# Attention and a routed feed-forward layer on one core: the front's instructions in a new order on four engines, and the second slot table partly moved between the first three rounds

## The reference

```python
def _L0_conv_ref(x, w_kq, b_kq, w_v, b_v, w_o, b_o):
    xf = x.reshape(B, C, N)
    kq = jnp.einsum('kc,bcn->bkn', w_kq, xf) + b_kq[None, :, None]
    v = jnp.einsum('vc,bcn->bvn', w_v, xf) + b_v[None, :, None]
    sim = jnp.einsum('bkn,bkm->bnm', kq, kq)
    attn = jax.nn.softmax(sim, axis=-1)
    ctx = jnp.einsum('bnm,bvm->bvn', attn, v)
    out = jnp.einsum('ov,bvn->bon', w_o, ctx) + b_o[None, :, None]
    ...
def _L0_ffn_ref(x, router_w, w1, w2, w3):
    logits = flat @ router_w.T
    probs = jax.nn.softmax(logits, axis=-1)
    topk_probs, topk_idx = jax.lax.top_k(probs, TOP_K)
    topk_probs = topk_probs / (jnp.sum(topk_probs, axis=-1, keepdims=True) + 1e-09)
    ...
    h = jax.nn.silu(h1) * h3
    y = jnp.einsum('neh,ech->nec', h, w2)
    out = jnp.einsum('ne,nec->nc', gates, y)
...
x = x + _L0_conv_ref(_ln_c(x), ...)
t = _to_tokens(x)
t = t + _L0_ffn_ref(_ln_t(t), ...)
```

## Time and profile before

| | us |
|---|---|
| median of 3 runs | 176.22 |
| lowest, highest | 175.45, 176.61 |
| the profiled execution's own time | 174.48 |
| its span (first to last instruction) | 172.7 |
| PE busy | 143.8 |
| DVE busy | 100.6 |
| POOL busy | 85.8 |
| ACT busy | 71.4 |

### The profile page before, as it was taken

The page is one execution under the profiler, slowest core; times in us unless marked ns, Lnnn a source line. Parts: engine busy times, 40 slices in busy tenths (PEclk is TensorE's granted clock), DMA queues, the critical chain, the costliest instruction groups (busy, mean ns, idle before and its releaser), DMA issues.

```text
span 172.7 us, 4880 instructions
## 1 busy us (share of the span) xinstructions
PE 143.8 (83%) x1682; PEld 120.2 (70%) x1682; DVE 100.6 (58%) x372; ACT 71.4 (41%) x141; POOL 85.8 (50%) x114
## 2 busy tenths in 40 slices
PE   1589849488788678996999999999999999983871
PEld 1356737277376258896798989999999999872271
DVE  1636695785853988869764656464555654532050
ACT  2347666141144044353363636363636354541021
POOL 2695237877770577773262626253444444466000
PEclk9999987955555589999999999999999999999698
DMA  4999300001872691298978889696949871010524
GB/s 136 313 292 295 101 0 23 27 15 35 268 308 48 217 348 52 58 320 296 318 278 275 323 258 344 235 358 184 393 111 395 266 281 37 9 34 16 160 106 109
DMA packets 19893, 33.00 MB, mean 191 GB/s; under 512 B 7691, under 2 KB 13100, under 8 KB 19868
## 3 DMA queue, kind: packets, MB, share of 16 engines
q1 hardware_dynamic: 16732, 29.55, 52.1%
q0 software_dynamic: 2272, 2.35, 4.1%
q10 hardware_dynamic: 864, 0.79, 1.4%
HBM read 25.55 MB, written 7.13 MB: 189 GB/s over the span
## 4 chain that ended last, share of the span: by engine, by line
PE 62%; DVE 9%; DMA 8%; issue 6%; ACT 5%; POOL 5%; SPq 1%; POOLq 1%; ACTq 0%; DVEq 0%
PE psum L1035 21%; PE psum L1063 12%; PE psum L929 7%; PE psum L918 4%; PE psum L1017 3%; POOL xs L361 3%; PE psum L898 3%; ACT xn L430 2%; DMA y_in<-ys 2%; PE psum L1041 2%; DMA x_in<-xs 2%; POOL ys L374 2%; PE psum L1107 2%; PE psum L889 2%; DVE hid L831 2%
## 5 line engine op out<-in xcount | busy, mean ns | idle before, releaser
L374 POOL DMA_INDIRECT ys<-y_out,y_row x39 | 37.4, 958 | 44.9 <-DVE hid L831 39.8
L831 DVE TENSOR_TENSOR hid<-psum,act_sb 128x512 f32<-128x512 f32 (+1 forms) x50 | 33.7, 677 | 29.4 <-ACT act_sb L508 28.7
L1035 PE MATMUL psum<-x_cols,weights 64*128 64x128 f32 x390 | 49.7, 279 | 0.3 <-ACT x_cols L500 0.2
L1037 PE MATMUL psum<-x_cols,weights 64*128 64x128 f32 x390 | 49.8, 279 | 0.0
L1035 PEld LDWEIGHTS psum<-x_cols,weights 64*128 64x128 f32 x390 | 45.6, 188 | 4.5 <-issue 2.2
L1037 PEld LDWEIGHTS psum<-x_cols,weights 64*128 64x128 f32 x390 | 45.6, 187 | 0.0
L508 ACT ACTIVATE act_sb<-psum 128x512 f32<-128x512 f32 (+1 forms) x50 | 29.3, 586 | 23.9 <-PE psum L1035 23.9
L361 POOL DMA_INDIRECT xs<-xrows,pos x32 | 31.7, 989 | 11.6 <-issue 8.9
L1063 PE MATMUL psum<-hid,weights 128*64 128x128 f32 x468 | 28.8, 276 | 0.2 <-DVE hid L831 0.2
L1063 PEld LDWEIGHTS psum<-hid,weights 128*64 128x64 f32 x468 | 25.9, 137 | 2.0 <-DVE hid L831 0.4
L929 PEld LDWEIGHTS psum<-u_sb,probsT 128*128 128x128 f32 x64 | 11.4, 268 | 5.2 <-ACT probsT L464 2.8
(11 more groups left out here) (148 smaller groups left out, 179.1 us busy)
## 6 DMA issues: line engine op xcount, KB each, us to landing
weights<-experts SPq DMA_DIRECT2D x39, 565.0 KB, 5.6
xs<-zeros SPq DMA_DIRECT2D x4, 1040.0 KB, 12.0
x_in<-xs SPq DMA_DIRECT2D x39, 32.5 KB
ys<-y_out,y_row POOLq DMA_INDIRECT x39
xs<-xrows,pos POOLq DMA_INDIRECT x32, 2.6
y_in<-ys ACTq DMA_DIRECT2D x2, 256.0 KB, 4.6
y_in<-ys SPq DMA_DIRECT2D x2, 256.0 KB, 4.4
x_sb<-x_tok SPq DMA_DIRECT2D x1, 384.0 KB, 3.6
```

Source lines behind the costliest of these rows:

```text
L374: nc.gpsimd.indirect_dma_start(ys, bass.IndirectOffsetOnAxis(ap=y_row[:, j:j + 1], axis=0), y_out[:, i % RING, h, :], None).then_inc(y_sca ...
L831: nc.vector.tensor_tensor(live(i, hid[:, i % 2, s, :]), live(i, H3_BANK[g % 3]), live(i, act_sb[:, g % 3, :]), ALU.mult).then_inc(hid_done, 1)
L1035: first_ = nc.tensor.matmul(H1_BANK[g % 2][:, src], weights[0:C, slot, P * s:P * (s + 1)], x_cols[0:C, i % 2, src], start=True, stop=True)
L1037: second_ = nc.tensor.matmul(H3_BANK[g % 3][:, src], weights[C:P, slot, P * s:P * (s + 1)], x_cols[C:P, i % 2, src], start=True, stop=True)
```

## The change

The work is the same; its order is another.

- PE: the similarities of the next pair stand between a pair's two attentions, not after them. `rank(p-1)` stands behind `value_out(p)` and also waits for the copy of these values. Transposes and keys of the pair after next stand at the pair's end. There are 23 `keep_busy` products in place of 14 up to the first quad.
- ACT: `xT_copy` moves behind the second image's probsT copy, next to `kq_copy`.
- DVE: `row_max` of the next pair's first image stands before the second residual, that of its second image before `positions`. The first table is split around residual(4), tops(4) and row_max(6). Behind the front, `rows_of_slots(1)`, `normalise_t(3)` and the parts of the third table move to places between the multiplies of quads 0, 1 and 2; `pair_up(2)` moves into quad 1.
- POOL: `t_deviation` stands before another scatter. `turn_x(2)` on PE and its copy on ACT move from quad 1's step 0 to its step 4.

```diff
+DEVIATION_AT = (4, 5, 3)
...
+        def turns_at(i):
+            return {0: 1, 1: 4}.get(i, 0)
...
             for p in range(PAIRS):
                 for at in range(TPP * K_TOP):
-                    if p == 0 and at == TPP * K_TOP - 2 or p == 2 and at == K_TOP:
+                    if p + 1 < PAIRS and at == DEVIATION_AT[p]:
                         t_deviation(p + 1)
                     scatter_row(p, at)
-                if p == 1:
-                    t_deviation(2)
...
                 u_copy(p)
-                if p + 2 < PAIRS:
-                    xT_copy(p + 2)
                 exponentials(2 * p + 1)
                 probsT_copy(2 * p + 1)
                 if p + 2 < PAIRS:
+                    xT_copy(p + 2)
                     kq_copy(p + 2)
...
             for p in range(PAIRS):
+                last = p == PAIRS - 1
+                if p >= 1:
+                    x_logits(p)
                 if p == KNOWN[0]:
                     subtiles_of_experts(0)
+                residual(2 * p)
+                tops(2 * p)
+                if not last:
+                    row_max(2 * p + 2)
+                if p == KNOWN[0]:
                     owners_of_slots(0)
                     rows_of_slots(0)
-                if p >= 1:
-                    x_logits(p)
-                residual(2 * p)
-                tops(2 * p)
                 residual(2 * p + 1)
                 t_statistics(p)
-                if p + 1 < PAIRS:
-                    row_max(2 * p + 2)
                 tops(2 * p + 1)
                 choose(p)
-                carry_on(p)
-                if p == PAIRS - 1:
+                if last:
                     pair_up(0)
+                else:
+                    carry_on(p)
+                    row_max(2 * p + 3)
                 positions(p)
-                if p == PAIRS - 1:
-                    used_up(0)
-                    subtiles_of_experts(1)
-                    owners_of_slots(1)
-                    rows_of_slots(1)
-                    pair_up(1)
-                normalise_t(p)
-                if p + 1 < PAIRS:
-                    row_max(2 * p + 3)
+                if not last:
+                    normalise_t(p)
+            pair_up(1)
+            used_up(0)
+            subtiles_of_experts(1)
+            owners_of_slots(1)
...
             def tables_between(i, s):
-                if (i, s) == (0, 5):
+                if (i, s) == (0, 1):
+                    rows_of_slots(1)
+                elif (i, s) == (0, 5):
+                    normalise_t(PAIRS - 1)
+                elif (i, s) == (1, 1):
                     used_up(1)
+                elif (i, s) == (1, 2):
                     subtiles_of_experts(2)
-                elif (i, s) == (1, 1):
+                elif (i, s) == (1, 5):
                     owners_of_slots(2)
-                elif (i, s) == (1, 3):
+                elif (i, s) == (2, 1):
                     rows_of_slots(2)
-                elif (i, s) == (1, 5):
+                elif (i, s) == (2, 5):
                     occupancy(2)
...
+                    if (i, s) == (1, 3):
+                        pair_up(2)
                     tables_between(i, s)
-                if i + 2 < NQ:
+                if 1 <= i < NQ - 2:
                     pair_up(i + 2)
...
+            def ranks_read(n):
+                pe.wait_ge(rank_read, n)
+                if n >= KNOWN[0]:
+                    pe.wait_ge(counts_ready, sum(k <= n for k in KNOWN))
...
-                pe.wait_ge(u_ready, p + 1)
+                pe.wait_ge(u_ready, min(p + 2, PAIRS))
...
             attend(0)
+            similarity(1)
             attend(1)
-            similarity(1)
             transpose_x(2)
             key_query(2)
             for p in range(1, PAIRS):
-                if p >= 2:
-                    keep_busy(3)
+                transpose_probs(2 * p)
+                if p == PAIRS - 1:
+                    keep_busy(4)
+                value_out(p)
                 rank(p - 1)
-                transpose_probs(2 * p)
-                value_out(p)
+                attend(2 * p)
+                transpose_probs(2 * p + 1)
+                if p + 1 < PAIRS:
+                    similarity(p + 1)
+                attend(2 * p + 1)
                 if p + 2 < PAIRS:
                     transpose_x(p + 2)
-                attend(2 * p)
-                transpose_probs(2 * p + 1)
-                if p + 2 < PAIRS:
                     key_query(p + 2)
-                attend(2 * p + 1)
-                if p + 1 < PAIRS:
-                    similarity(p + 1)
-            keep_busy(4)
+                elif p + 1 < PAIRS:
+                    keep_busy(7)
+            keep_busy(8)
             rank(PAIRS - 1)
             keep_busy(3)
```

More of the change, by code:

```diff
@@ L531, in _ @@
                     silu(STEPS * i + s)
-                    if s == (1 if i == 0 else 0) and i + 1 < NQ:
+                    if s == turns_at(i) and i + 1 < NQ:
                         columns(i + 1)
@@ L894, in value_out @@
                     pe.wait_ge(t_ready, 2 * p)
-                    pe.wait_ge(rank_read, p)
-                    pe.wait_ge(counts_ready, sum(k <= p for k in KNOWN))
+                    if p >= 2:
+                        ranks_read(p - 1)
                 for i in range(TPB):
@@ L926, in attend @@
                     pe.wait_ge(t_ready, b - 1)
+                if b >= 2 and b % 2 == 1:
+                    ranks_read(b // 2)
                 for i in range(2):
@@ L938, in rank @@
                     pe.wait_ge(carry_ready, p)
-                    pe.wait_ge(rank_read, p)
-                    pe.wait_ge(counts_ready, sum(k <= p for k in KNOWN))
-                pe.wait_ge(u_ready, p + 1)
+                    ranks_read(p)
+                pe.wait_ge(u_ready, min(p + 2, PAIRS))
                 pe.wait_ge(t_ready, 2 * (p + 1))
```

## The result

The changed kernel takes 189.44 us (median of four runs, 186.98 to 191.9) against 175.83 of the kernel before (174.59 to 176.61); the ratio is 1.0739, interval 1.0669 to 1.0809. A second set gave 1.0652 (1.0568 to 1.0735). On 176.4 that is 11.5 to 13.0 us lost; the forecast was 9.1. Of the range of 180 to 189, 188.8 (1.0739 times 175.83) lies inside near the top, the second set's median of 188.0 too, and the first set's median of 189.44 just above. They answer to the earlier trace rows.

A forecast was written before the change was run, and what follows sets the result against it. After the front, time was quad 0's start, 3.8 us lost in two quads, and 8.98 per dense quad. Quad 4, on the later of rows and weights, starts 9.1 late: 183.6 us, or 185.3 on 176.22; range 180.0 to 189.0.

The forecast's parts named there:

- steps 1 and 2: Front: pair 1's ranks read at 40.3 against 35.13; first table ends at 46.9 against 40.00.
- step 6: Third table ends at 94.0 against 81.77; SP waits, and quad 4 starts at 110.7, 9.1 us late.
- One sign of being right: Turn_x(4), in quad 3 on PE, would idle on x_pairs for 3 us or more.
- steps 5 and 6: Slowest weights land in 7.6: quad 2's in place at 87.9, quad 4's chain giving 110.3 by weights, 110.7 by rows.
- the 16.0: From the first table's end to quad 0's rows in place: 16.0 us, so rows at 62.9.
- Rival C: PE idles before quad 0, runs part of it at 1.2 GHz, both scatter waits stay: +12, 188.2 us; chance 0.12.
- The 2.9 at pair_up(0): Slack of the chain from first table to quad 0's rows before DVE's pair_up(0): only 2.9 us.
- The weighing of the scatter wait: SP's wait for pair 1's last scatters before the first rows: between 0 and 1.0, taken as 0.
- A: Front runs at the high clock; only the late third table costs, +4.9: 181.1 us; chance 0.22.
- B: Faster: quads 0 and 1 lose their 3.8 us of PE idling, giving 172.4 us; chance 0.04.
- D: First table keeps its slack, later tables hide behind SP's queue: within 2 us of 176.2; chance 0.04.
- Costed at nothing: Nine dummy matmuls (up to 3.8 us uncovered), turn_x(2) and pair_up(2) moved (0 to 1), POOL's deviations moved: 0.

The follow-up runs named there:

- e1: Changed kernel with only the third table's parts back at their old places: 182.91 us, ratio 1.0354 to the kernel before.
- e2: Kernel before with only the third table's owners, rows and occupancy at their new places: 183.32 us, ratio 1.0417.
- e5: Changed kernel with 24 keep_busy products in place of 3 ahead of turn_x(0): ratio 1.0668 to the kernel before.
- e8: Kernel before with the whole first table moved behind x_logits(2), residual(4) and tops(4): 178.84 us, ratio 1.0127.
- e4: Changed kernel with third table at its old places, first table in one piece, pair 2's deviation behind pair 1's scatters: 178.58 us, ratio 1.0175 to the kernel before.
- e6: Changed kernel with the third table, turn_x(2), its copy and pair_up(2) at their old places: 181.43 us, ratio 1.0312 to the kernel before.
- e3: Changed kernel, third table still late, with first table in one piece and pair 2's deviation behind pair 1's scatters: 187.29 us, ratio 1.062 to the kernel before.
- e7: Kernel before with next pair's similarities ahead of the second attention, both row maxima early, 10 keep_busy products before pair 1's ranks: 176.27 us, ratio 0.9963.

## Why the forecast was right, and where it was off

**Direction and cause.** Both hold. The first table is late by the new place of the ranks and what stands inside it (steps 1 and 2, each within 0.5). The late third table stops SP, and quad 4 starts late (step 6), which e1 and e2 show from both sides: 3.3% with the front late (1.070, the mean of the two sets, over 1.0354), 4.2% without. One sign of being right did not come: turn_x(4) was to idle 3 us or more for quad 4's rows, and idled 1.26. From the third table to these rows doubled it took 6.5 (96.15 to 102.68), not 8.7, as the last row load was in place 1.7 after its issue, not 3.8. PE stood for quad 4's weights instead, 2.95, the way that step 6 had ending 0.4 earlier (110.3). That the rows came at 102.68, where the sum had 102.7, is luck: a table 2.15 later than forecast and a way 2.2 shorter.

**The size.** The forecast had quad 4 at 110.7; it started at 113.64. The step that failed is the 7.6 for the slowest weights in steps 5 and 6: they took 8.83 and 8.47, in e2 8.82. That is 2.1 of the 2.9. The 7.6 was misread: the view behind the earlier trace rows counts a load only if all its landing marks are in the trace, 20 of the 39, so its maximum is no bound. For quad 4's four loads in the changed kernel it gives this, while the chain has the last of them at 8.47:

```profile
DMA to landing us min/median/max: 4.1/6.5/7.5
```

In the trace of the kernel before, the last landing mark of quad 4's fourth load stands 8.77 after its start, so for step 6 the weights had not become slower; quad 2's fourth load did take 7.6 there. Of the other 0.8, 0.5 came with the first table; the first rows took 0.65 more than the 16.0, and quad 1's rows gave that back. Behind quad 4 two terms were missing altogether: quad 4's 10.46 in place of 8.98, 1.5, behind its wait, and the last 32 products ahead of the output, 5.35 in place of 3.84, at a mean granted clock of 0.70 in place of 1.00. No run ties the second to the change. Rival C had priced the clock, but put it at quad 0, where e5 shows no cost. The two profiled executions lie 187.4 - 172.7 = 14.7 apart, the medians 12, as the old one was under its median and this one above.

**The slack.** The 2.9 at pair_up(0) were read as the only way from the first table to the end. In e8 the table was 4.15 late and pair_up(0) still had no wait, so the rows need less than table + 15.5 there; the loss came by SP's scatters instead. A first table 4.15, 5.05 and 6.95 late (e8, e4, e1) cost 2.2, 3.1 and 6.2. In the first two about 2 are free, and what lies beyond is paid; in e1 0.75, or 2.2 if the 1.5 of quad 7 are left out. That is a summary of three runs, not a mechanism of its own.

**The weighing of the scatter wait.** The prediction took 0, as by its reading of the rule in the Trainium skill's DMA: Bandwidth & Descriptors, section "Queues, rings and completion order" (queues in turn, a packet at a time). This kernel does not bear that reading out: 5.7 against 2.2 with and without weights in flight. Whether the queues take turns or not, no run here shows. In the changed kernel this cost SP 0.7, as weights went out ahead of pair 1's last scatters; small beside its wait for the second and third table (first row), of which there was 5.8 before, for the second alone:

```profile
SPq L293 <- DVE table L709: 11.5, 2, 6.4
...
SPq L301 <- DMA xs<-xrows,pos: 0.7, 1, 0.7
```

**The rivals.** A: the front did get the high clock, from 48.9 on, but the first table stands at 47.39, so it came too late to help; the fall came at 25, after PE had stood 2.6 for exponentials(2). B: quads 0 and 1 took 23.61, more than the 21.77 before; in e2, with the front in time, they did give back 2.1 of the 3.8, and the third table took more. C: right that PE would idle ahead of quad 0 (5.05) and start it slowly; that this costs, e5 does not bear out. D: e2 shows it false.

**Costed at nothing.** The dummy products cost nothing: DVE waited 5.57 at pair_up(0) behind them. Turn_x(2) stood 2.23, which quad 2's weights cover in the changed kernel (they end 1.79 later still); once they do not, e6 differs from e1 by 0.7, which is within the noise. The deviation's place was not tried alone.

## What to carry to other kernels

Follow each table or index that a load queue waits for to the last transfer issued from it, and ask how far that queue is ahead of its consumer at that point: here about 2 us by e8 and e4, and a third table 7.6 later (e2, 89.36 for 81.77) stops the products. A queue without lead also eats gains made upstream: 3.3 us won in the front (e3) were 0.6 to 2.1 at the end, by which set of the changed kernel one takes. And moving a maximum or a similarity forward need not pay while another engine's chain releases the next step: in e7 PE waited 3.65 for DVE's choices, and no gain could be told.

## What the runs showed that was not expected

- Scatters by index wait behind bulk loads: 5.7 us from start to landing with weights on the way, 2.2 without. Where a queue waits for scatters, large loads issued just ahead of them are on the path.
- A short wait can cost more than itself: after 2.95 at quad 4 and 1.8 in quad 7 (e3), PE ran at 1.2 GHz for a while, which cost about 1.5 each. It need not: after 2.61 at quad 4 in e3 and 1.79 at quad 2 of the changed kernel the clock stayed at 1.00. The low clock at quad 0's start showed no cost, as DVE was the later one.
- Four weight loads of a quad needed 10.4 and 10.7 us from the first issue to the start of the quad that waited for them (10.8 at quad 4 in e2). In the kernel before, where none waited, quad 4's landed 10.3 after the first issue by the last landing mark: a landing row that leaves loads out is no upper bound.
- The row loads of quad 4 behaved like the scatters: the last was in place 3.8 us after its issue with weights on the way (4.2 in e4), and 1.7 in the changed kernel (1.9 in e2 and in e3), where the third table is late and SP had issued the last weights 9 us before. No run changed this alone.
